# Four scans of 128 tiles: a loop of turns in each direction, or one straight block for each

## The reference

```python
xz = x @ w_in.T
xi, z = jnp.split(xz, 2, axis=-1)
...
xc = silu(xc)                       # after a 3x3 depthwise convolution, 256 channels
...
xs = jnp.concatenate([x_hwwh, jnp.flip(x_hwwh, axis=-1)], axis=1)
x_dbl = jnp.einsum('bkdl,kcd->bkcl', xs, x_proj_w)
dts, Bs, Cs = jnp.split(x_dbl, [DT_RANK, DT_RANK + D_STATE], axis=2)
...
def step(h, inp):
    d_t, x_t, B_t, C_t = inp
    dA = jnp.exp(d_t[..., None] * As)
    h = dA * h + (d_t * x_t)[..., None] * B_t[:, :, None, :]
    y = jnp.einsum('bkdn,bkn->bkd', h, C_t)
    return (h, y)
```

## Time and profile before

| | |
|---|---|
| median of 3 runs | 29705.68 us (29699.24 to 29705.95) |
| the profiled execution's own time | 29696.74 us |
| its span from first to last instruction | 29695.1 us |
| mean granted TensorE clock | 0.966 of full speed |
| first product of the scans (L1154) | 5397.23 us |
| last product of the scans | 28650.41 us |

### The profile page before, as it was taken

The page is one execution under the profiler, slowest core; times in us unless marked ns, Lnnn a source line. Parts: engine busy times, 40 slices in busy tenths (PEclk is TensorE's granted clock), DMA queues, the critical chain, the costliest instruction groups (busy, mean ns, idle before and its releaser), DMA issues. The chain is left out here.

```text
span 29695.1 us, 503466 instructions
## 1 busy us (share of the span) xinstructions
PE 24898.3 (84%) x178572; PEld 20517.0 (69%) x178572; DVE 25338.3 (85%) x26926; ACT 25459.9 (86%) x50840; POOL 23052.8 (78%) x16524
## 2 busy tenths in 40 slices
PE   4999977888888888888888888888888888888877
PEld 2888844677777776777777677777776777777765
DVE  7666678888989898989899898989998989899975
ACT  2444434899999999999999999999999999999975
POOL 0000000799999999999999999999999999999961
PEclk7998978999999999999999999999999999999998
DMA  4101022333333333333333333333333333333333
GB/s 152 31 27 39 28 89 77 111 119 116 116 115 119 115 118 123 130 129 131 129 129 131 123 131 128 133 128 131 128 132 124 130 128 132 127 132 128 131 124 130
DMA packets 1456172, 3408.57 MB, mean 115 GB/s; under 512 B 98208, under 2 KB 1149248, under 8 KB 1173952
## 3 DMA queue, kind: packets, MB, share of 16 engines
q1 hardware_dynamic: 1453632, 3375.95, 32.0%
HBM read 2921.54 MB, written 454.03 MB: 114 GB/s over the span
## 5 line engine op out<-in xcount | busy, mean ns | idle before, releaser
L1120 DVE TENSOR_TENSOR_SCAN s_h<-s_da,s_h,s_db 128x512 f32<-128x512 f32 x16384 | 19688.8, 1261 | 1916.0 <-PE s_db L1020 1598.8
L1154 POOL TENSOR_TENSOR s_prod<-s_h,s_cb 128x1024 f32<-128x1024 f32 x8192 | 19578.1, 2390 | 170.9 <-DVE s_h L1120 91.3
L1020 PE MATMUL s_db<-eye,s_dxb 128*128 128x128 f32 x65536 | 8768.0, 277 | 3524.6 <-issue 1902.7
L1020 PEld LDWEIGHTS s_db<-eye,s_dxb 128*128 128x128 f32 x65536 | 7117.6, 141 | 5860.3 <-issue 4690.9
L1083 ACT ACTIVATE s_da<-s_delta,a_neg 128x512 f32<-128x512 f32 x16384 | 10924.7, 721 | 2.7 <-DVE s_h L1120 2.7
L1072 ACT ACTIVATE s_dxb<-s_dx,s_btok 128x256 f32<-128x256 f32 x24576 | 10708.0, 507 | 109.9 <-issue 65.8
L1033 PE MATMUL s_py<-eye,s_prod 128*128 128x128 f32 x65536 | 8498.3, 273 | 44.2 <-POOL s_prod L1154 44.2
L1033 PEld LDWEIGHTS s_py<-eye,s_prod 128*128 128x128 f32 x65536 | 7427.5, 141 | 55.5 <-POOL s_prod L1154 55.5
L1136 POOL TENSOR_SCALAR s_dxb<-s_dx,s_btok 128x256 f32<-128x256 f32 x8192 | 4073.6, 497 | 248.6 <-POOLq L56 165.1
L734 POOL COPY c_xi<-c_xi 128x1032 f32<-128x1032 f32 x8 | 8.4, 1046 | 5345.0 <-DVEq L626 5345.0
L480 DVE SCALAR_TENSOR_TENSOR a_sc<-a_scores,a_bias 128x512 f32<-128x512 f32 x1024 | 683.5, 689 | 690.3 <-PE a_scores L370 690.3
(11 more groups left out here) (136 smaller groups left out, 20448.2 us busy)
## 6 DMA issues: line engine op xcount, KB each, us to landing
s_cb<-c_rows SPq DMA_DIRECT2D x2048, 1024.0 KB, 4.7
s_xt<-xc_tok SPq DMA_DIRECT2D x1024, 256.0 KB, 5.2
y<-s_yt SPq DMA_DIRECT2D x1024, 256.0 KB
s_yb<-y SPq DMA_DIRECT2D x768, 256.0 KB, 5.2
xc_tok<-c_ot SPq DMA_DIRECT2D x32, 2048.0 KB, 7.5
o_y<-y SPq DMA_DIRECT2D x64, 1024.0 KB, 6.1
n_x<-in_x SPq DMA_DIRECT2D x64, 512.0 KB, 5.4
zn_t<-n_zt SPq DMA_DIRECT2D x32, 1024.0 KB, 7.3
```

Of the source, the lines that this page charges most:

```text
L1020: last = e.transpose(db[:, i % NDB, half, j * P:(j + 1) * P], dxb[:, i % NDXB, j, half * P:(half + 1) * P], const["eye"][:, :])
L1120: last = e.tensor_tensor_scan(h[:, n, half, flow], da[:, i % NDA, half, flow], db[:, i % NDB, half, flow], h[:, n, half, last_token:last_t ...
L1154: e.tensor_tensor(prod[:, i % NP_], h[:, n], cb[:, n, :].unsqueeze(1).to_broadcast([P, HALVES, T]), ALU.mult).then_inc(S["prod"], 1)
```

## The change

`scan_phase`, called four times, becomes `scans_phase`, called once. The tiles in SBUF and PSUM are allocated once for all directions. There is one block with the table load and one that prepares tile 0 of direction 0. Then follow four blocks, one for each direction (`one_direction`), each with all 128 tiles written out; there is no loop. In the last tile of directions 0 to 2 the 13 stages prepare tile 0 of the next direction, with that direction's weights (`weights`) and from its own view of `xc_tok` (`load_tile`). `h` is not cleared: the scans of tile 0 take 0.0 as initial value. DRAM addresses are constants. The steps themselves, the buffers, the depths and the order within an engine stay. `prepare_act` gets `skips`, which stands for k == 0 of the direction in whose tile it runs.

```diff
-def scan_phase(nc, sems, k, xc_tok, c_rows, y_before, y_k, wts, const):
+def scans_phase(nc, sems, xc_tok, c_rows, ys, wts, const):
...
-    N = 32
...
-    STEPS = N * D_STATE
-    backwards = k >= 2
-    by_column = k % 2 == 1
-    flow = slice(None, None, -1) if backwards else slice(None)
-    last_token = 0 if backwards else T - 1
+    STEPS = TILES * D_STATE
+    backwards = lambda k: k >= 2
+    by_column = lambda k: k % 2 == 1
...
-        if by_column:
-            view = lambda t: t.rearrange("(b p w) d -> w p b d", b=JB, p=P)
-        else:
-            view = lambda t: t.rearrange("(i b p) d -> i p b d", b=JB, p=P)
-        src, dst = view(xc_tok), view(y_k)
-        before = view(y_before) if k else None
+        def lines(t, k):
+
+            if by_column(k):
+                return t.rearrange("(b p w) d -> w p b d", b=JB, p=P)
+            return t.rearrange("(i b p) d -> i p b d", b=JB, p=P)
 
         with nc.Block() as block:
-            @block.vector
-            def _(e):
-                e.memset(h[:, :, :, last_token], 0.0)
-
...
-        def line(it, g, i):
-
-            tile = (TILES - 1 - g) - it * N if backwards else it * N + g
-            return tile * LINES + i
-
-        def load(e, it, g):
+        def line(k, g, i):
+
+            return ((TILES - 1 - g) if backwards(k) else g) * LINES + i
+
+        def load(e, k, g):
             for i in range(LINES):
-                e.dma_start(xt[:, g % 2, i * JB:(i + 1) * JB, :], src[line(it, g, i)]).then_inc(S[f"load{g % 2}"], DMA)
+                e.dma_start(xt[:, g % 2, i * JB:(i + 1) * JB, :], lines(xc_tok, k)[line(k, g, i)]).then_inc(S[f"load{g % 2}"], DMA)
...
-        def prepare_pe(e, g, n, stage, alone):
+
+        def prepare_pe(e, w, g, n, stage, alone):
             s = g % 2
             if stage == 0:
...
-                    last = e.matmul(pr[0:ROWS_LOW, 0, :], wts["proj"][:, half, :], xc[:, s, half, :],
+                    last = e.matmul(pr[0:ROWS_LOW, 0, :], w["proj"][:, half, :], xc[:, s, half, :],
...
-        def prepare_act(e, g, n, stage):
+        def prepare_act(e, w, g, n, stage, skips):
             s = g % 2
             if stage == 1:
                 e.wait_ge(S["turned"], n)
-                if k == 0 and n >= 2:
+                if skips and n >= 2:
                     e.wait_ge(S["skipped"], n - 1)
...
-        def one_turn(it, last_turn):
+        def one_direction(k):
+            flow = slice(None, None, -1) if backwards(k) else slice(None)
+            last_token = 0 if backwards(k) else T - 1
+
             def prepares(g):
 
-                return 1 <= g and (g < N or (g == N and not last_turn))
+                return 1 <= g and (g < TILES or (g == TILES and k + 1 < DIRECTIONS))
+
+            def weights(g):
+                return wts[k] if g < TILES else wts[k + 1]
+
+            def load_tile(e, g):
+                if g < TILES:
+                    load(e, k, g)
+                else:
+                    load(e, k + 1, g - TILES)
...
@@ -973,39 +977,39 @@
                         if g >= 1:
                             e.wait_ge(S["added"], g)
                         for i in range(LINES):
-                            e.dma_start(yb[:, i * JB:(i + 1) * JB, :], before[line(it, g, i)]).then_inc(S[f"before{g % 2}"], DMA)
+                            e.dma_start(yb[:, i * JB:(i + 1) * JB, :], lines(ys[k - 1], k)[line(k, g, i)]).then_inc(S[f"before{g % 2}"], DMA)
 
                     def store(g):
                         e.wait_ge(S["y"], 2 * (g + 1))
                         for i in range(LINES):
-                            e.dma_start(dst[line(it, g, i)], yt[:, i * JB:(i + 1) * JB, :]).then_inc(S[f"store{g % 2}"], DMA)
-
-                    load(e, it, 1)
+                            e.dma_start(lines(ys[k], k)[line(k, g, i)], yt[:, i * JB:(i + 1) * JB, :]).then_inc(S[f"store{g % 2}"], DMA)
+
+                    load_tile(e, 1)
                     load_c(e, 0, CGROUPS - 1)
-                    load(e, it, 2)
+                    load_tile(e, 2)
                     if k:
                         load_before(0)
-                    for g in range(N):
+                    for g in range(TILES):
                         if g >= 1 and prepares(g + 2):
                             e.wait_ge(S["dx"], g)
-                            load(e, it, g + 2)
+                            load_tile(e, g + 2)
                         if g >= 1:
                             store(g - 1)
                         if prepares(g + 1):
                             store_c(e, g + 1, g + 1)
                             e.wait_ge(S["cstore"], DMA * (g + 1))
                         for q in range(CGROUPS):
-                            if prepares(g + 1) and (q < CGROUPS - 1 or g + 1 < N):
+                            if prepares(g + 1) and (q < CGROUPS - 1 or g + 1 < TILES):
                                 e.wait_ge(S["prod"], g * D_STATE + (q + 1) * GROUP)
                                 load_c(e, g + 1, q)
-                            if q == 2 and k and g + 1 < N:
+                            if q == 2 and k and g + 1 < TILES:
                                 load_before(g + 1)
-                    store(N - 1)
+                    store(TILES - 1)
                     for s in range(2):
-                        e.wait_ge(S[f"store{s}"], LINES * DMA * (N // 2))
-                    if prepares(N):
+                        e.wait_ge(S[f"store{s}"], LINES * DMA * (TILES // 2))
+                    if prepares(TILES):
                         for q in range(CGROUPS - 1):
-                            e.wait_ge(S[f"cl{q}"], DMA * N)
+                            e.wait_ge(S[f"cl{q}"], DMA * TILES)
...
-                            prepare_pe(e, g + 1, g + 1, n, False)
+                            prepare_pe(e, weights(g + 1), g + 1, g + 1, n, False)
...
-                                                scale=wts["a_neg"][:, half, n:n + 1])
+                                                scale=wts[k]["a_neg"][:, half, n:n + 1])
...
-                            prepare_act(e, g + 1, g + 1, n)
+                            prepare_act(e, weights(g + 1), g + 1, g + 1, n, k == 0)
...
+                            first = h[:, n, half, last_token:last_token + 1] if g else 0.0
                             last = e.tensor_tensor_scan(h[:, n, half, flow], da[:, i % NDA, half, flow], db[:, i % NDB, half, flow],
-                                                        h[:, n, half, last_token:last_token + 1], ALU.mult, ALU.add)
+                                                        first, ALU.mult, ALU.add)
                         last.then_inc(S["h"], 1)
                         if prepares(g + 1):
-                            prepare_dve(e, g + 1, g + 1, n)
+                            prepare_dve(e, weights(g + 1), g + 1, g + 1, n)
...
-        turns = TILES // N
-        with nc.Fori(0, turns - 1) as it:
-            one_turn(it, False)
-        one_turn(turns - 1, True)
+        for k in range(DIRECTIONS):
+            one_direction(k)
...
-        for k in range(DIRECTIONS):
-            own = {n: wts[n][k] for n in per_direction + ("a_neg", "guard_less_dt_b")}
-            scan_phase(nc, sems, k, xc_tok, c_rows, ys[k - 1] if k else None, ys[k], {**wts, **own, "guard": guard, "d_diag": d_diag}, const)
+        own = [{n: wts[n][k] for n in per_direction + ("a_neg", "guard_less_dt_b")} for k in range(DIRECTIONS)]
+        scans_phase(nc, sems, xc_tok, c_rows, ys, [{**o, "guard": guard, "d_diag": d_diag} for o in own], const)
```

More of the change, by code:

```diff
@@ L778, in scan_phase @@
     SUBS_ACT = 3
-    STEPS = N * D_STATE
-    backwards = k >= 2
-    by_column = k % 2 == 1
-    flow = slice(None, None, -1) if backwards else slice(None)
-    last_token = 0 if backwards else T - 1
+    STEPS = TILES * D_STATE
+    backwards = lambda k: k >= 2
+    by_column = lambda k: k % 2 == 1
     with ExitStack() as stack:
         m = Memory(nc, stack)
[L786 to L801, removed]
+        xt = m.sb("s_xt", [P, 2, SUBS, D_INNER])
+        xc = m.sb("s_xc", [P, 2, HALVES, T])
+        low = m.sb("s_low", [ROWS_LOW, T])
+        btok = m.sb("s_btok", [P, 2, SUBS, D_STATE])
+        delta = m.sb("s_delta", [P, 2, HALVES, T])
+        dx = m.sb("s_dx", [P, 2, SUBS, D_INNER])
+        dxb = m.sb("s_dxb", [P, NDXB, SUBS, D_INNER])
+        da = m.sb("s_da", [P, NDA, HALVES, T])
+        h = m.sb("s_h", [P, D_STATE, HALVES, T])
+        cb = m.sb("s_cb", [P, D_STATE, T])
+        prod = m.sb("s_prod", [P, NP_, HALVES, T])
+        yt = m.sb("s_yt", [P, SUBS, D_INNER])
+        yb = m.sb("s_yb", [P, SUBS, D_INNER])
+        db = m.ps("s_db", [P, NDB, HALVES, BANK])
+        py = m.ps("s_py", [P, 2, BANK])
+        pr = m.ps("s_pr", [P, 2, BANK])
         flat = lambda t: t.rearrange("p a b -> p (a b)")
@@ L870, in prepare_pe @@
                 last.then_inc(S["turnb"], 1)
```

(27 more changed lines are left out.)

## The result

The changed kernel takes 29446.28 us (median of 6 runs, 29432.56 to 29455.50), the kernel before 29702.07 us (6 runs); the ratio is 0.9914, 95% interval [0.9901, 0.9926]. The profiled execution took 29435.48 us, 261.3 less than the one of before.

A forecast was written before the change was run, and what follows sets the result against it. GpSimd was taken as the full engine in the scans, so boundary pauses are lost: 179.1 us inside directions plus 76.8 us at changes, 255.9 us off 29705.7, gives 29449.8 us; range 29422 to 29478.

The forecast's parts named there:

- The bound: Scans: GpSimd is busy throughout interior windows in directions 1 to 3, so time lost at a block's end is not regained.
- Part 1: Scans: removing the loop removes the twelve block boundaries inside directions, saving 179.1 us.
- The instruction supply's part: Loop's jumps back in the scans: 8 times 3.57 us, 29 us of the 179.
- Part 2: Three changes of direction: each shrinks to the cost of a loop exit into straight code, saving 76.8 us.
- this edit: First scans on DVE: immediate 0.0 in place of a cleared column, put at nothing; without cover 16 us more or less.
- Sum: Whole kernel: 179.1 + 76.8 = 255.9 us saved, from 29705.7 to 29449.8 us, 0.86% less.
- Pace unchanged in long straight code: Interior tiles: straight and looped turns run at the same pace; unknown left is 28 us either way.
- rival (b): Straight blocks of 128 tiles: instructions come late, 3.46 us a stall; one every two tiles gives 30336 us; chance 0.04.
- Rival (a): Changes of direction stay as expensive, only boundaries inside directions are gained: 29526.6 us; chance 0.05.

The follow-up runs named there:

- half product: The changed kernel with GpSimd's product over one of the two halves of channels only, the other left zero: 29184.15 us, 0.9825 of the kernel before.
- blocks of 8: The changed kernel cut into straight blocks of 8 tiles without a loop, 60 boundaries more: 30196.09 us, 1.0163 of the kernel before.
- blocks of 32: The changed kernel cut into straight blocks of 32 tiles without a loop, twelve boundaries more: 29632.51 us, 0.9965 of the kernel before.
- all in one block: The changed kernel with all 512 tiles of the four directions in one straight block: 29434.04 us on the first chip, 29409.97 us on the second.
- the loop with the new change: The kernel before, loop kept, with a direction's last tile preparing the next direction's first and DVE clearing h's column: 29660.92 us, 0.9976.

## Why the prediction was right

- **The bound.** "An engine that is full cannot make up for a pause": the half product shows that GpSimd is that engine in directions 1 to 3, and the blocks of 8 tiles show that 60 pauses add up in full. The rule reached further than its reason: direction 0 leaves GpSimd 19 us of 1359, and a boundary costs about the same there.
- **Part 1, 179.1 us for twelve boundaries inside directions.** Alone it measured 175.5 us by the medians, 179.0 by the kernel's own tiles.
- **The instruction supply's part, 29 us of it.** The loop against straight blocks of the same length: 28.4 us by the medians, 176.0 - 146.8 = 29.2 by their own tiles.
- **Part 2, 76.8 us for three changes of direction.** Alone (with the loop kept) it measured 67.6 us by the medians, 77.9 by the kernel's own tiles; in the changed kernel 114.7 - 34.9 = 79.8. Each change was priced as an exit of the loop, which takes 1462.91 - 32 x 45.323 = 12.6 us over its tiles in direction 0, then 12.2 and 13.0. It took 11.1, 12.1 and 11.7: the saving was put 3 us too low in all. The pause between products was forecast at 12 to 13 us and came out at 11.3 to 11.7. About one of the three lies in the rows that it was priced from: the twelve straight boundaries of the blocks of 32 cost 12.2 us on average, and these three exits 12.6. Another piece is in the trace. Scans whose initial value is an immediate, a constant held in the instruction, are shorter than the others; the line of the scans in the changed kernel:

```profile
L1125 DVE TENSOR_TENSOR_SCAN s_h<-s_da,s_h,s_db x16256: 1245/1256/1284, 5446.0 to 28392.7; 128x512 f32<-128x512 f32 x199
L1125 DVE TENSOR_TENSOR_SCAN s_h<-s_da,s_db x128: 1194/1196/1222, 5401.2 to 22716.5; 128x512 f32<-128x512 f32 x128
```

  60 ns each (medians 1196 and 1256 ns). I had put this edit at nothing because DVE has room in a tile; but right behind a barrier two of these scans are on GpSimd's path (its wait for them is 3.58 us, 3.70 and more in the earlier trace rows). That is a tenth of a microsecond a boundary; where the remaining 1.5 us or so are stays open.
- **Sum.** 255.9 us predicted; 255.8 by the medians (29702.07 to 29446.28), 261.55 in the windows of the two profiled executions, 294.4 - 34.9 = 259.5 by the tiles' own times. The agreement of the medians is closer than the method deserves: another pair, on another chip, gave 264.3. That the median fell within 4 us of 29449.8 is in part luck, since medians of one kernel and its windows differ here by more.
- **Pace unchanged in long straight code.** Interior tiles within 0.3 us in 1340, so rival (b) has nothing to stand on: "issue" ahead of GpSimd's products is 81.1 us against 79.4, and ACT has none. It grew a little for TensorE's transposes to `db` (1934.8 us against 1902.7), which doesn't reach the pace.
- **Rival (a)**, changes of direction as expensive as before, would have shown in a wait of the first scalings, or for the first tile's load. The barrier's 6.34 us and the scan's 3.58 us are all there is.

## What to carry to other kernels

Where one engine is full, price a block boundary by windows from the first instruction of one block to the first of the next, minus the interior pace times the tiles: the difference holds drain, store wait, barrier, refill and halting start in one number. Here that was 11 to 13 us for a straight boundary, 15 to 17 with a loop's jump back (1444.61 - 32 x 44.652 = 15.7 in direction 1), and 36 to 40 with a preparation phase of its own, each paid in full. Prepare the next phase's first tile in this phase's last one, and, if the program's length allows, leave the boundary out altogether: the semaphores that order the steps can order the phases too.

## What the runs showed of the hardware that I had not expected

The pace of the tiles has two levels in the kept profiles, 0.1% apart. The same kernel (all in one block), the same 30 tiles of direction 1, first on the first chip, then on the second:

```profile
11244.54:12585.65 1341.11, 1145.97 (x8762) 969.49 (x8760) 1229.77 (x1081) 1332.79 (x2671) 1341.11 (x961) 1.00 0.37 131
```

```profile
11253.00:12592.50 1339.50, 1145.61 (x8759) 969.54 (x8758) 1228.45 (x1081) 1332.46 (x2671) 1339.50 (x961) 1.00 0.37 131
```

1.61 us in 30 tiles are 27 us in 512, about the 24.1 us between its medians on the two chips. It isn't the chip alone, nor the kernel alone: on the first chip the profiled execution of the loop with the new change had the short window (1339.43 us), that of the straight blocks of 32 the long one (1340.98).

```profile
11307.69:12647.12 1339.43, 1145.24 (x8759) 969.12 (x8758) 1227.96 (x1081) 1333.81 (x2672) 1339.43 (x961) 1.00 0.37 131
```

```profile
11314.44:12655.42 1340.98, 1146.02 (x8762) 969.65 (x8760) 1229.80 (x1081) 1333.32 (x2673) 1340.98 (x961) 1.00 0.37 131
```

On the second chip the blocks of 8 had the long tiles (22989 us in all, by the table above) and the changed kernel the short ones (22959). That one kernel changes its level from one execution to the next on the same chip isn't shown, as only one execution of each was profiled there. The prediction's range of 28 us either way, taken from the difference between two directions, happened to be the size of this. Why there are two levels stays open. The phases outside the scans vary too: what follows the last product took 1044.70 us before, 1038.60 in the changed kernel and 1057.80 in the loop with the new change, with the same code. Differences below some 30 us between two single executions of this kernel mean nothing until windows over the part in question say the same.
